# An attention and Fourier-mixer kernel: the weighted sum of the previous step stands on TensorE behind the third pair of tiles of a step, in place of behind the second

## The chip, the cores and the metric

One core of a Trainium2 chip runs the whole program. The metric is the device time of one execution in microseconds (us). Before the change the median of three runs is 1471.29 us (1470.57 to 1473.84). The execution that was profiled took 1468.0 us, of which 1466.2 us lie between the first and the last instruction.

## The reference, cut to what matters

```python
def _L0_conv_ref(x, w_qkv, w_o):           # 8 images of 1024 tokens, 192 channels
    qkv = xt @ w_qkv                       # 12 heads of 16
    attn = softmax(einsum('bhqd,bhkd->bhqk', q, k) * scale)
    out = einsum('bhqk,bhkd->bhqd', attn, v)
    out = out.swapaxes(1, 2).reshape(bs, n, c) @ w_o
...
def _L1_conv_ref(x, w1, b1, w2, b2, bias_w, bias_b):
    bias = x @ bias_w.T + bias_b
    xf = rfftn(x in 4 blocks of 48 channels, axes=(1, 2))
    ...                                    # two small complex layers per frequency, relu between
    return irfftn(...) + bias
...
x = x + _L0_conv_ref(_gn(x), ...)          # _gn: group norm over 32 groups
x = x + _L1_conv_ref(_gn(x), ...)
```

## The kernel before, in words

The program goes through eight images (`b`), and TensorE does each image in 48 steps (`u`, from 0), 16 for each of three groups of four heads. A step has four score tiles, `score_tile(b, g, s, 0..3)`, each of 128 keys by 512 queries for one head; ScalarE takes the exponential of each into `probs`. The score tiles rotate through three banks, so score tile n waits for the exponential of tile n-3.

A step also has four max tiles, `max_tile` 0 to 3. They are tiles of the same products for a stretch of work 11 steps ahead, and VectorE takes the maximum of each row (`take_max`, L1053). They rotate through a ring of four banks, together with everything else that needs a bank: the "pieces". `bank_free` makes TensorE wait until the entry four places earlier in the ring was read out.

TensorE runs a score tile and a max tile in the two halves of its rows at once, so the tiles come in pairs. This document calls them A (max 0 with score 0), B (max 1 with score 1), C (score 2 with max 2) and D (score 3 with max 3). Each reads 48 or 50 rows, and so do, with 64 rows, the small products `qk`, `v`, `proj` and `lin` (all L1340). Everything else on TensorE uses its full height.

The weighted sum of a step, `pv` (W in this document, L1317), multiplies the probabilities of its four score tiles by v and adds into `o_acc`. It is done one step late: W of step u-1 stands in step u. Its four products lie beside each other in the array's columns and use all 128 rows.

The pieces prepare the next image ("prep": turn, mean, var, qk, v) and finish the image before ("post": proj, turn, mean, var, spread, dftw, dfth, mix1, mix2, idfth, idftw, lin). The tables `PREP_AT` and `POST_AT` give for each step the pieces ahead of pair A (START) and those in the middle of the step (MID); `qk`, `v`, `proj` and `lin` come two at a time. With full height, these stand in the middle: prep `var` in step 11, post `var` in 19, `dftw` 2 in 27, `dfth` 0 and 1 in 30, `idftw` 1 in 6 and `idftw` 3 in 7. The `v` pieces of steps 32 and 37 stand there too. `qk` pieces stand ahead of pair A in steps 17, 19, 23, 27 and 32. Each `qk` piece is read out twice: ScalarE copies it (L967), then VectorE subtracts the rounded copy (L1106), and only then is the bank free. The `lin` and `proj` pieces are read by VectorE, the `v` pieces by ScalarE (L961).

Steps 3, 8, 20, 21, 24 and 43 have no pieces. Transposes of the joined row maxima (L1304, `turn_shift`) stand behind pair D of steps 5, 13, 21, 29, 37 and 45. VectorE does the pieces ahead of pair A before the row maxima 0 and 1 of the step. ScalarE does a step in the order: pieces ahead of A, exponentials 0 and 1, at the first step of a group the copy of `o_acc` (`take_o`, L949), MID pieces, exponentials 2 and 3. At the ninth step of a group `take_o` comes first. In all, the loop runs 384 steps. All engines run their instructions in program order, which is written out by hand as shown.

Of the kernel before, what the change touches and what calls it, by code (L numbers as in the profile page):

```python
# [47 lines left out]
START, MID = 0, 1  # L48
# [210 lines left out]
def build(nc, consts, x, w_qkv, w_o, w1, b1, w2, b2, bias_w, bias_b, out):  # L259
# [3 lines left out]
    with ctx:  # L263
# [139 lines left out]
        def after(eng, s, count):  # L403

            if not isinstance(count, int) or count > 0:
                eng.wait_ge(s, count)
# [56 lines left out]
        def ring_bank(entry):  # L463
            return ring[:, RING_NO[entry] % RING, :]
# [26 lines left out]
        def pieces_of(b, u, part, prep, post):  # L491

            late = post and not (isinstance(b, int) and b < 2)
            return [e for e in pieces_at(u, part)
                    if (prep if e[0] == "prep" else late if e[1] == 2 else post)]
# [24 lines left out]
        def max_unit(unit, i):  # L520

            half, m = divmod(unit, HUNITS)
            hp, qt = divmod(m, NT // 2)
            return half, hp, qt, 1 - i % 2, i // 2

        def max_bank(b, g, unit, i):

            if b == 0 and g == 0 and unit < AHEAD:
                return ring[:, i, :]
            return ring_bank(("max", (STEPS * g + unit - AHEAD) % IN_BODY, i))  # L530
# [13 lines left out]
        def halves(b, g, half):  # L544

            return 2 * NG * b + 2 * g + half
# [696 lines left out]
        def _(pe):  # L1243
            mm = nc.tensor.matmul

            def score_tile(b, g, s, h):
                n = g * TILES + s * GH + h
                half, kt = divmod(s, NT)
                if kt == 0 and h == 0:
                    pe.wait_ge(shift_in, 64 * (halves(b, g, half) + 1))  # L1250

                after(pe, probs_made, NG * TILES * b + n + 1 - SCORE_BANKS)
                hp, odd = divmod(h, 2)
                rows = slice(64 * odd, 64 * odd + KQ + 2)
                mm(scores[:, n % SCORE_BANKS, :], k_stack[rows, 2 * g + hp, P * kt:P * (kt + 1)],  # L1255
                   q_stack[rows, g, half, hp, :],
                   start=True, stop=True).then_inc(scores_made, 1)

            def bank_free(b, entry):

                held = bank_held(b, entry)
                if held is None:
                    return
                of, (which, *what) = held
                if isinstance(of, int) and of < 0:
                    pe.wait_ge(max_taken, 4 * (AHEAD - 1) + RING_NO[entry] % RING + 1)
                    return
                if which == "max":
                    g, unit = divmod(what[0] + AHEAD, STEPS)
                    pe.wait_ge(max_taken, TILES * (NG * of + g) + 4 * unit + what[1] + 1)  # L1270
                if which == "turned":
                    pe.wait_ge(shift_split, 2 * halves(*next_half(of, what[0])) + 2)
                if which == "prep":
                    prep_taken(pe, of - what[0], *what[1:])
                if which == "post" and isinstance(of, int) and of == 0:
                    pe.wait_ge(setup_taken, SETUP_TAKEN[SETUP_IN.index(held[1])])
                elif which == "post":
                    post_taken(pe, of - what[0], *what[1:])

            def max_tile(body, u, slot, b, g, unit, i):  # L1280
                half, hp, qt, odd, which = max_unit(unit, i)
                no = 4 * unit + i
                if unit == 0 and i == 0:
                    pe.wait_ge(stacked[g], STACK_INCS * (b + 1))
                if unit == HUNITS and i == 0:
                    pe.wait_ge(stacked_second[g], SECOND_INCS * (b + 1))

                if body == -1:
                    after(pe, max_taken, no + 1 - RING)
                else:  # L1290
                    bank_free(body, ("max", u, i))
                rows = slice(64 * odd, 64 * odd + KQ)
                mm(max_bank(b, g, unit, i),  # L1293
                   q_stack[rows, g, half, hp, P * qt:P * (qt + 1)],
                   k_stack[rows, 2 * g + hp, HALF * which:HALF * (which + 1)],
                   start=True, stop=True).then_inc(max_made, 1)
# [252 lines left out]
            def body(b, prep, post):  # L1549
                first = isinstance(b, int) and b == 0  # L1550

                def pieces(u, part):
                    for which, back, kind, k in pieces_of(b, u, part, prep, post):
                        entry = (which, back, kind, k)
                        bank_free(b, entry)
                        if kind not in PAIRED:
                            (prep_piece if which == "prep" else post_piece)(
                                b - back, kind, k, ring_bank(entry))
                        elif k % 2:
                            (prep_pair if which == "prep" else post_pair)(  # L1560
                                b - back, kind, k, (ring_bank((which, back, kind, k - 1)),
                                                    ring_bank(entry)))
                    for stage, bank_ in setup_of(u, part, first):
                        bank_free(b, SETUP_IN[stage - 1])
                        setup(stage, bank_)

                for u in range(IN_BODY):
                    g, s = divmod(u, STEPS)
                    tiles = unit_ahead(b, u, prep)
                    pieces(u, START)  # L1570
                    for tile in tiles[0:1]:
                        max_tile(b, u, *tile)
                    score_tile(b, g, s, 0)
                    for tile in tiles[1:2]:
                        max_tile(b, u, *tile)
                    score_tile(b, g, s, 1)
                    if s > 0:
                        pv(b, g, s - 1)
                    elif g > 0:
                        pv(b, g - 1, STEPS - 1)  # L1580
                    elif not first:
                        pv(b - 1, NG - 1, STEPS - 1)
                    pieces(u, MID)
                    score_tile(b, g, s, 2)
                    for tile in tiles[2:3]:
                        max_tile(b, u, *tile)
                    score_tile(b, g, s, 3)
                    for tile in tiles[3:]:
                        max_tile(b, u, *tile)
                    if u in shift_steps(prep):  # L1590
                        turn_shift(b, u, *next_half(b, u))
# [74 lines left out]
```

## Time and profile before

| what | value |
|---|---|
| runs, median (lowest to highest) | 1471.29 us (1470.57 to 1473.84) |
| profiled execution | 1468.0 us, span 1466.2 us |
| mean granted TensorE clock | 0.984 |
| TensorE matmul busy | 1402.4 us, 96% |
| VectorE busy | 1153.8 us, 79% |
| ScalarE busy | 1010.8 us, 69% |
| GpSimd busy | 187.9 us, 13% |

Matmul records overlap (two of a pair run at once, and their ends are modelled), so the distance from one start to the next says more than the length of a record. A row of the timeline merges consecutive records of one kind on one engine: its start, the time to the end of the last of them, and behind the shapes how many there are. A product in plain float32 has two records, a pair's tile one.

### The profile page before, as it was taken

The numbers are of one execution on the slowest core, as the hardware profiler recorded it, in microseconds if no ns is written. First come the engines' busy times: TensorE is split into PE (matmuls) and PEld (weight loads), VectorE is DVE, ScalarE is ACT, GpSimd is POOL, SyncE is SP. The second block draws the span as 40 slices with busy tenths as digits, with TensorE's granted clock in tenths as the row PEclk, the third lists the DMA queues.
The fourth block names the chain that finished last, engine by engine and source line by source line (L and its number), as shares of the span: only waits on it lengthen the run. The fifth ranks groups of instructions, "written<-read, shape, count | busy, mean of one in ns | idle before, by whom it ended". The sixth has DMA issues, their size and how long they took to land.

```text
span 1466.2 us, 27125 instructions
## 1 busy us (share of the span) xinstructions
PE 1402.4 (96%) x9852; PEld 668.4 (46%) x9852; DVE 1153.8 (79%) x2123; ACT 1010.8 (69%) x2018; POOL 187.9 (13%) x277
## 2 busy tenths in 40 slices
PE   7899989999999999999999999999999999999977
PEld 4434333444444444444545454444445454434454
DVE  4788888997799878987799878988799878988041
ACT  1166777777767777777777777677777777677712
POOL 2000000040011200140001300140010400040000
PEclk8699999999999999999999999999999999999999
DMA  6610321233530533323422524324432424311323
GB/s 127 88 25 11 79 73 34 52 91 67 109 84 22 106 85 75 74 73 76 104 74 45 107 68 88 80 58 78 109 71 43 87 74 85 88 33 44 82 44 89
DMA packets 100605, 106.35 MB, mean 73 GB/s; under 512 B 24760, under 2 KB 77560, under 8 KB 100472
## 3 DMA queue, kind: packets, MB, share of 16 engines
q1 hardware_dynamic: 98584, 102.98, 32.6%
q10 hardware_dynamic: 1888, 1.63, 0.6%
q8 instruction: 79, 1.29, 0.4%
q14 instruction: 54, 0.44, 0.1%
HBM read 26.99 MB, written 6.67 MB: 23 GB/s over the span
## 4 chain that ended last, share of the span: by engine, by line
PE 81%; DVE 10%; issue 2%; ACT 2%; DMA 1%; POOL 1%; ACTq 0%; SPq 0%; DVEq 0%; POOLq 0%
PE o_acc L1317 23%; PE ring L1293 16%; PE scores L1255 15%; PE ring L1340 10%; DVE row_max L1053 8%; PE ring L1329 3%; PE ring L1451 2%; PE ring L1444 2%; PE ring L1438 2%; PE ring L1357 2%; PE ring L1430 2%; PE ring L1457 1%; DVE qk_parts L1106 1%; ACT probs L941 1%; PE scores L1340 1%
## 5 line engine op out<-in xcount | busy, mean ns | idle before, releaser
L1053 DVE TENSOR_REDUCE row_max<-ring 128x1 f32<-128x512 f32 x1536 | 973.4, 682 | 173.1 <-PE ring L1293 166.9
L941 ACT ACTIVATE probs<-scores 128x512 f32<-128x512 f32 x1536 | 830.0, 599 | 253.9 <-PE scores L1255 252.4
L1293 PE MATMUL ring<-k_stack,q_stack 48*128 48x512 f32 x1536 | 597.3, 465 | 27.8 <-DVE row_max L1053 17.1
L1255 PE MATMUL scores<-q_stack,k_stack 50*128 50x512 f32 x1536 | 598.3, 462 | 1.3 <-ACT probs L941 1.2
L1317 PE MATMUL o_acc<-probs,v_aug 128*18 128x512 f32 x3072 | 406.2, 601 | 4.7 <-ACT o_raw L949 3.6
L1255 PEld LDWEIGHTS scores<-q_stack,k_stack 50*128 50x128 f32 x1536 | 244.3, 185 | 312.6 <-ACT probs L941 298.2
L1293 PEld LDWEIGHTS ring<-k_stack,q_stack 48*128 48x128 f32 x1536 | 248.3, 187 | 153.3 <-DVE row_max L1053 103.9
L584 POOL TENSOR_TENSOR inv_all<-o_raw,inv_all 128x1024 f32<-128x1024 f32 x23 | 54.5, 2371 | 565.0 <-DMA inv_all<-inv_rows 565.0
L1317 PEld LDWEIGHTS o_acc<-probs,v_aug 128*18 128x18 f32 x3072 | 52.0, 96 | 124.1 <-issue 83.8
L1340 PE MATMUL ring<-xt,w_qk 64*128 64x256 f32 x540 | 69.2, 385 | 0.8 <-DVE xt L1092 0.8
L1340 PEld LDWEIGHTS ring<-xt,w_qk 64*128 64x128 f32 x540 | 54.2, 189 | 11.8 <-DVE row_max L1053 3.8
L967 ACT CAST qk_parts<-ring 128x256 fp32r<-128x256 f32 x90 | 29.4, 375 | 41.6 <-PE ring L1340 40.6
L1106 DVE TENSOR_TENSOR qk_parts<-ring,qk_parts 128x256 fp32r<-128x256 f32 x90 | 34.1, 416 | 25.0 <-ACT qk_parts L967 24.6
L881 POOL COPY v_aug<-v_new 128x512 f32<-128x512 f32 x24 | 14.4, 621 | 243.8 <-ACT v_new L961 213.9
L981 ACT COPY rows_a<-ring 128x384 f32<-128x384 f32 x59 | 28.5, 484 | 19.6 <-PE ring L1457 9.6
L836 POOL TENSOR_TENSOR calc<-mean_var,calc 128x1 f32<-128x1 f32 x16 | 3.1, 191 | 299.5 <-DVE calc L1128 212.8
L1451 PE MATMUL ring<-mix_b,spec_a 97*128 97x96 f32 (+1 forms) x304 | 37.2, 274 | 0.7 <-ACT spec_a L989 0.7
L1451 PEld LDWEIGHTS ring<-mix_b,spec_a 97*128 97x128 f32 (+1 forms) x304 | 33.2, 176 | 8.5 <-issue 7.4
L1125 DVE TENSOR_TENSOR x<-ring,x 128x192 f32<-128x192 f32 x60 | 18.7, 352 | 23.0 <-PE ring L1340 23.0
L1438 PE MATMUL ring<-cst,rows_b 128*96 128x128 f32 x240 | 33.2, 286 | 3.3 <-DMA rows_b<-rows_a 3.3
L1340 PE MATMUL ring<-bias_t,xt 64*128 64x192 f32 x360 | 36.3, 326 | 0.0
L1340 PE MATMUL ring<-wo,o_t 64*128 64x192 f32 x366 | 35.2, 322 | 1.0 <-DVE tok_n L1132 1.0
(159 smaller groups left out, 1020.2 us busy)
## 6 DMA issues: line engine op xcount, KB each, us to landing
k_stack<-qk_parts SPq DMA_DIRECT2D x144, 128.0 KB, 4.4
q_stack<-qk_parts SPq DMA_DIRECT2D x285, 64.0 KB, 2.2
inv_all<-inv_rows SPq DMA_DIRECT2D x23, 512.0 KB
rows_b<-rows_a SPq DMA_DIRECT2D x122, 96.0 KB, 3.0
x_in<-in_x_dram SPq DMA_DIRECT2D x8, 768.0 KB, 5.3
x_res<-in_x_dram SPq DMA_DIRECT2D x8, 768.0 KB, 5.3
spec_b<-spec_a SPq DMA_DIRECT2D x60, 102.0 KB, 2.3
o_t<-inv_all SPq DMA_DIRECT2D x184, 32.0 KB, 2.3
```

The source lines that it names most:

```text
L584: ops.tensor_tensor(inv_all[:, :], o_raw[:, :], inv_all[:, :], ALU.mult).then_inc(o_normed, 1)
L941: nc.scalar.activation(probs[:, GH * (s % 2) + h, :], scores[:, n % SCORE_BANKS, :], ACT.Exp, scale=SCALE).then_inc(probs_made, 1)
L967: nc.scalar.copy(qk_parts[:, 0, PARTS[k // 4], token_quarter(k)], bank_[:, 0:QUARTER]).then_inc(part0_done, 1)
L1053: nc.vector.tensor_reduce(row_max[:, which, m:m + 1], max_bank(b, g, unit, i), AX.X, ALU.max).then_inc(max_taken, 1)
L1106: nc.vector.tensor_tensor(qk_parts[:, 1, PARTS[k // 4], cols], bank_[:, 0:QUARTER], qk_parts[:, 0, PARTS[k // 4], cols].bitcast(F32), ALU. ...
L1255: mm(scores[:, n % SCORE_BANKS, :], k_stack[rows, 2 * g + hp, P * kt:P * (kt + 1)], q_stack[rows, g, half, hp, :], start=True, stop=True). ...
L1293: mm(max_bank(b, g, unit, i), q_stack[rows, g, half, hp, P * qt:P * (qt + 1)], k_stack[rows, 2 * g + hp, HALF * which:HALF * (which + 1)], ...
L1317: last = mm(o_acc[32 * h:32 * h + VW, 0, :], v_aug[:, g, kt, h, :], probs[:, GH * (s % 2) + h, :], start=(kt == 0), stop=(kt == NT - 1), s ...
L1329: last = mm(bank_[ROWS * half:ROWS * (half + 1), P * t:P * (t + 1)], src[:, t + NT // 2 * half, third::THIRDS], ident, start=True, stop=True)
L1340: out.append(mm(banks[half][:, 0:n], lhs, rhs, start=(c == 0), stop=(c == 2)))
L1438: last = mm(bank_[0:CH, P * n:P * n + f.shape[1]], rows_b[:, j, CH * chunk:CH * (chunk + 1)], f, start=True, stop=True)
L1451: last = mm(to[:, :, blk, :], hidden[:, blk, P * k:P * k + n], mix_b[:, blk, :], start=True, stop=True)
```

## The change

In the TensorE part of `body`, the MID pieces, score tile 2 and max tile 2 move ahead of the weighted sum. Nothing is added or taken away, and no other engine's order changes.

```diff
                     for tile in tiles[1:2]:
                         max_tile(b, u, *tile)
                     score_tile(b, g, s, 1)
+                    pieces(u, MID)
+                    score_tile(b, g, s, 2)
+                    for tile in tiles[2:3]:
+                        max_tile(b, u, *tile)
                     if s > 0:
                         pv(b, g, s - 1)
                     elif g > 0:
                         pv(b, g - 1, STEPS - 1)
                     elif not first:
                         pv(b - 1, NG - 1, STEPS - 1)
-                    pieces(u, MID)
-                    score_tile(b, g, s, 2)
-                    for tile in tiles[2:3]:
-                        max_tile(b, u, *tile)
                     score_tile(b, g, s, 3)
```

A step was `[START] A B W [MID] C D` and is `[START] A B [MID] C W D`.

Step 27 of an image in the middle of the program, on TensorE: `qk` products (L1340), pairs A and B, W (L1317), `dftw` 2 (L1430), pairs C and D. Before:

```order
L1340 MATMUL ring<-xt,w_qk 128x256 x6
L1293 MATMUL ring<-k_stack,q_stack 128x512
L1255 MATMUL scores<-q_stack,k_stack 128x512
L1293 MATMUL ring<-k_stack,q_stack 128x512
L1255 MATMUL scores<-q_stack,k_stack 128x512
L1317 MATMUL o_acc<-probs,v_aug 18x512 x4
L1430 MATMUL ring<-tok_n,cst 128x384
L1255 MATMUL scores<-q_stack,k_stack 128x512
L1293 MATMUL ring<-k_stack,q_stack 128x512
L1255 MATMUL scores<-q_stack,k_stack 128x512
L1293 MATMUL ring<-k_stack,q_stack 128x512
```

And of the changed kernel, the same place:

```order
L1340 MATMUL ring<-xt,w_qk 128x256 x6
L1293 MATMUL ring<-k_stack,q_stack 128x512
L1255 MATMUL scores<-q_stack,k_stack 128x512
L1293 MATMUL ring<-k_stack,q_stack 128x512
L1255 MATMUL scores<-q_stack,k_stack 128x512
L1430 MATMUL ring<-tok_n,cst 128x384
L1255 MATMUL scores<-q_stack,k_stack 128x512
L1293 MATMUL ring<-k_stack,q_stack 128x512
L1317 MATMUL o_acc<-probs,v_aug 18x512 x4
L1255 MATMUL scores<-q_stack,k_stack 128x512
L1293 MATMUL ring<-k_stack,q_stack 128x512
```

The `dftw` product now stands between two pairs, and W between two others.

Step 32 of the same image on TensorE, in the changed kernel: `qk` products, A, B, the `v` products (L1340, `wv`), C, W, D, and then the first `dfth` products (L1438) of step 33. Before, the row of L1317 stood directly ahead of the row with `wv`.

```order
L1340 MATMUL ring<-xt,w_qk 128x256 x6
L1293 MATMUL ring<-k_stack,q_stack 128x512
L1255 MATMUL scores<-q_stack,k_stack 128x512
L1293 MATMUL ring<-k_stack,q_stack 128x512
L1255 MATMUL scores<-q_stack,k_stack 128x512
L1340 MATMUL ring<-wv,xt 128x192 x6
L1255 MATMUL scores<-q_stack,k_stack 128x512
L1293 MATMUL ring<-k_stack,q_stack 128x512
L1317 MATMUL o_acc<-probs,v_aug 18x512 x4
L1255 MATMUL scores<-q_stack,k_stack 128x512
L1293 MATMUL ring<-k_stack,q_stack 128x512
L1438 MATMUL ring<-cst,rows_b 96x128 x7
```

The `v` products are now directly behind pair B, and the last thing ahead of pair D is W.

## Rows read from the trace of the kernel before

**Rows 1.** The page: span, busy time and share of each engine, instructions.

```profile
span 1466.2 us, 27125 instructions
PE 1402.4 (96%) x9852; PEld 668.4 (46%) x9852; DVE 1153.8 (79%) x2123; ACT 1010.8 (69%) x2018; POOL 187.9 (13%) x277
```

**Rows 2.** Timeline of TensorE, fifth image, from pair C of step 2.

```profile
740.93 0.50 PE L1255 MATMUL scores<-q_stack,k_stack 50*128 50x512 f32 x1
...
741.27 0.62 PE L1255 MATMUL scores<-q_stack,k_stack 50*128 50x512 f32 x2
741.50 0.62 PE L1293 MATMUL ring<-k_stack,q_stack 48*128 48x512 f32 x2
742.11 0.50 PE L1255 MATMUL scores<-q_stack,k_stack 50*128 50x512 f32 x1
742.60 1.05 PE L1317 MATMUL o_acc<-probs,v_aug 128*18 128x512 f32 x8
743.58 0.50 PE L1255 MATMUL scores<-q_stack,k_stack 50*128 50x512 f32 x1
...
743.92 0.39 PE L1255 MATMUL scores<-q_stack,k_stack 50*128 50x512 f32 x1
744.25 1.12 PE L1329 MATMUL ring<-cst,x_in 128*64 128x128 f32 x16
```

**Rows 3.** Timeline of ScalarE, the same stretch; in brackets idle time before.

```profile
741.46 2.07 ACT L941 ACTIVATE probs<-scores 128x512 f32<-128x512 f32 x4 [0.75 <-PE scores L1255]
```

**Rows 4.** Timeline of TensorE, step 2 of that image: A, B and W.

```profile
739.02 0.53 PE L1255 MATMUL scores<-q_stack,k_stack 50*128 50x512 f32 x1
...
739.52 0.49 PE L1255 MATMUL scores<-q_stack,k_stack 50*128 50x512 f32 x1
739.94 1.05 PE L1317 MATMUL o_acc<-probs,v_aug 128*18 128x512 f32 x8
```

**Rows 5.** Timeline of VectorE, the same step.

```profile
738.17 1.29 DVE L1053 TENSOR_REDUCE row_max<-ring 128x1 f32<-128x512 f32 x2 [0.30 <-PE ring L1293]
739.39 0.62 DVE L1125 TENSOR_TENSOR x<-ring,x 128x192 f32<-128x192 f32 x2
```

**Rows 6.** Timeline of TensorE, fourth image, step 23: B and D.

```profile
643.14 0.40 PE L1255 MATMUL scores<-q_stack,k_stack 50*128 50x512 f32 x1
...
644.79 0.40 PE L1255 MATMUL scores<-q_stack,k_stack 50*128 50x512 f32 x1
```

**Rows 7.** Timeline of VectorE, the same step.

```profile
643.62 0.76 DVE L1106 TENSOR_TENSOR qk_parts<-ring,qk_parts 128x256 fp32r<-128x256 f32 x2 [0.72 <-ACT qk_parts L967]
644.29 2.48 DVE L1053 TENSOR_REDUCE row_max<-ring 128x1 f32<-128x512 f32 x4
```

**Rows 8.** Timeline of TensorE, step 27: B, then the middle piece.

```profile
655.60 0.40 PE L1255 MATMUL scores<-q_stack,k_stack 50*128 50x512 f32 x1
...
656.90 0.91 PE L1430 MATMUL ring<-tok_n,cst 128*128 128x384 f32 x2
```

**Rows 9.** Timeline of VectorE, step 27.

```profile
656.18 0.75 DVE L1106 TENSOR_TENSOR qk_parts<-ring,qk_parts 128x256 fp32r<-128x256 f32 x2
```

**Rows 10.** Timeline of TensorE, step 32: B, the `v` products, the next step's `dfth`.

```profile
673.58 0.40 PE L1255 MATMUL scores<-q_stack,k_stack 50*128 50x512 f32 x1
...
674.95 1.21 PE L1340 MATMUL ring<-wv,xt 64*128 64x192 f32 x11
...
676.61 0.57 PE L1438 MATMUL ring<-cst,rows_b 128*96 128x128 f32 x3
```

**Rows 11.** Timeline of ScalarE, step 32: `take_o`, then the `v` pieces.

```profile
675.07 0.62 ACT L949 COPY o_raw<-o_acc 128x512 f32<-128x512 f32 x1
676.24 0.54 ACT L961 COPY v_new<-ring 128x192 f32<-128x192 f32 x2 [0.55 <-PE ring L1340]
```

**Rows 12.** Timeline of TensorE, fourth image, step 9: W and its wait.

```profile
595.32 1.05 PE L1317 MATMUL o_acc<-probs,v_aug 128*18 128x512 f32 x8 [0.43 <-ACT o_raw L949]
```

**Rows 13.** Waits of the whole span: who, for whom, us in total, times, longest.

```profile
PEld ring L1293 <- DVE row_max L1053: 103.9, 253, 1.6
```

## The prediction

> **What bounds the kernel now.** I read the page first: TensorE is busy 96% of the span, VectorE 79% [rows 1]. Then the timeline of TensorE by starts, since its records overlap, and beside it the timelines of VectorE and ScalarE to see who frees a bank when. Last the table of waits.
>
> The reader is to see a fixed cadence in the starts [rows 2]. C starts at 740.93, D at 741.27: 0.34 us, as the first pair behind something of full height. The next pair follows 0.23 behind (741.50). From the last pair of a run to a full-height product it is 0.33 (743.92 to 744.25). From W to the next pair it is 0.98 (742.60 to 743.58). So a run of n pairs between full-height products costs 0.67 + 0.23 (n - 2), and to cut one run in two costs 0.34 + 0.33 - 2 x 0.23 = 0.21 us; a run of one pair is 0.44 by this (0.42 seen, 739.52 to 739.94 [rows 4]). W and the pairs never run together.
>
> TensorE still waits in two kinds of step, both times at B. In steps without pieces the run is C D A B, and B's score tile needs the exponential of C's: it starts at 742.11, 0.61 behind its forerunner instead of 0.23, just behind the first of the four exponentials that began at 741.46, 0.59 each by the distance of scores [rows 2, 3]. W follows at 742.60, 0.05 later than a lone pair asks for, held by D's exponential. In steps that begin with two small products (`proj`, `lin`), B starts 0.50 behind A (739.02, 739.52), because its bank is that of the previous D, whose maximum ends at 739.46 [rows 4, 5]. So a bank freed is a pair started 0.06 later. W stands behind B and waits with it.
>
> **The change, part by part.** It moves each W behind C, and with that the MID pieces ahead of W. No work is added. I count per image, against the 1468.0 us of the profiled execution.
>
> *Runs.* With full-height pieces at START, the runs {C D} {A B} become {D} {A B C}: two runs and four pairs either way, so 0. Without them C D A B becomes D A B C, one run either way, 0. A full-height MID piece stood beside W and cut nothing; now it stands between B and C, and a third run appears: 0.21 each. There are 40 such places in the program (7 images each for `var`, `var`, `dftw` 2, `dfth`; 6 for the two `idftw`): 8.4 us if nothing else happens.
>
> By the Trainium skill, TensorEngine Tiling (Array Packing), Key Properties, a change of tiling mode drains TensorE. The change adds one switch of mode at each of these places, as my count of runs does; if the drain were the pair's 0.50 record less 0.23, the 40 places would cost 10.8 us in place of 8.4.
>
> *Steps without pieces.* In the run D A B C, C's score tile needs the exponential of D's, which is again the first of the run. The wait moves from B to C with its size; only W's own 0.05 goes. Cycle before: 742.60 - 740.93 + 0.98 = 2.65; after: 1.18 + 0.44 + 0.98 = 2.60 [rows 2]. Gain 0.05 in six steps.
>
> *Small products at START.* D's maximum now has the whole run to be done, so B no longer waits (0.27). But C's max tile takes the bank of the first small product, and it comes 0.23 behind B instead of 1.2. VectorE reads the two in 0.62, from 739.39 [rows 5], so the first is free at 739.70, C starts at 739.76 instead of 739.48: 0.28 lost. Net 0 for eight `proj`/`lin` steps; two `v` steps gain 0.05 each. Where VectorE is behind its work at that moment (steps 13 and 29, with a normalisation ahead of them) I take 0.3 and 0.15 of loss; 0.13 for the `v` pieces of step 37.
>
> *`qk` at START.* Here the read-out is a ScalarE copy and then a VectorE subtraction. In step 23 B starts at 643.14, C could start at 643.37, but the first subtraction ends at 644.00 (643.62, two in 0.76) [rows 6, 7]. So C starts at 644.06, W at 644.50, D at 645.48; before, D started at 644.79. Loss 0.69. W used to lie on this wait and hide it; it is 0.98 long and the wait 0.7, so all of it was hidden. Late next: D's exponential, and with it C of step 24, by the same amount. The four row maxima that VectorE does from 644.29 on [rows 7] show that it is behind here, so part of the lateness is absorbed where TensorE waited for VectorE anyway: in steps 17 to 22 I take two `qk` losses of 0.70 and 0.77 (the latter with `var` and its cut), less 0.10 for two steps without pieces, less 0.27 twice for the waits at B of steps 18 and 22: 0.83. Steps 23 and 24: 0.69 - 0.05.
>
> *Step 27*, `qk` and `dftw` 2 in the middle: its bank is that of the first `qk` piece, free at 656.55 (656.18, two in 0.75) [rows 9]. Behind B (655.60) it could start at 655.93 [rows 8]; it starts at 656.61, and 0.21 for the cut: 0.89.
>
> *Step 32*, `qk` and `v` in the middle, is the dearest. The `v` products wait for both `qk` banks: 1.24 behind B as in step 23 (643.14 to 644.38), so 674.87 instead of 673.81. They take 0.98 with C's start at 675.85; W starts at 676.29, D at 677.27, the next piece at 677.7 instead of 676.61 [rows 10]. And this is the first step of a group: ScalarE's `take_o` waits for this W and the `v` copies queue behind it. Before, it started 1.17 behind W's start of 673.90 (675.07) and the copies were free of it. Now it starts at 677.46, ends at 678.05, the first `v` copy ends at 678.3 [rows 11], and the first `dfth` product of step 33, which takes that bank, starts at 678.4: 1.75 late.
>
> *MID elsewhere.* Step 7 loses 0.21. Steps 6, 11 and 30 lose 0.21 and get back the 0.2 that B waited there: 0.
>
> *Steps 8 and 9.* W of step 9 waited 0.43 for `take_o` [rows 12]. W of step 8 comes later, but D's exponential earlier relative to it, and C now stands ahead of W of step 9: 0.40 gained.
>
> Sum for an image with both kinds of pieces: 0.83 + 0.64 + 0.89 + 1.75 + 0.58 + 0.21 = 4.90 lost; 0.40 + 0.15 (steps 3, 8, 43) + 0.10 = 0.65 gained. Net 4.25 over seven images: 29.8 us, from which I take 2 because the first image has no post pieces, so that TensorE waits more there anyway and its step 33 needs no `v` bank. That makes 1468.0 + 28 = 1496; the median of the runs stands 3.3 above the profiled execution, and I say 1498.
>
> **Rivals.**
>
> *The moved wait is absorbed.* Everything late behind a `qk` piece is caught up where TensorE would have waited anyway, and only the 40 cuts cost: +8.4 - 3.2 for step 9 = 1471.3 + 5 = 1476. For it: VectorE is 79% busy and behind around steps 17 to 24. Against it: behind steps 27 and 32 come full-height steps with the bare cadence of rows 2, and there is no wait to fall into.
>
> *Faster.* The waits at B go and nothing takes their place, because C's max tile finds its bank free: VectorE gets to it sooner than I think, or C's score tile keeps the array busy alone. Ten steps with small products (0.27) and six without pieces (0.45) make 5.4 per image, 40 us over seven and a half: 1431. That TensorE waits for row maxima 253 times for 103.9 us [rows 13] leaves room for it. The point that decides is whether the bank of the first small product is free within 0.17 of B's start (C follows 0.23 behind B, and 0.06 of it are the release). I put it at 0.45 in the `lin` step (739.70 against a B at 739.25) and at 0.86 in the `qk` step (644.00 against 643.14), so `lin` is nearer to the edge [rows 4 to 7]. If only `lin` and `proj` gained, that is 8 x 0.27 x 7 = 15 us, and the sum would be 1483.
>
> *No change.* Losses and gains of some 15 us each cancel: 1471. Nothing ties them together.
>
> That the order does not change as said is excluded by the rows of order.
>
> **How the numbers follow.** Forecast as summed: 0.76, with a range of its own from 1484 (half of the loss of step 32, or all of the gain in `lin` steps) to 1508 (no absorption in steps 17 to 24, 0.54 an image or 4 us, and another 0.1 in the ten small-product steps of each image, 7 us). Absorbed: 0.12. Faster: 0.07. No change: 0.05. The range is 1476 to 1508: it takes in my own sum's low side and the middle of the absorbed case, and leaves the two rivals below out. A difference of 0.2% is about what a measurement of this kernel can tell from no change. The part of the absorbed case and of my own that falls below is small: faster 0.08, same 0.06, slower 0.86.
>
> **What the profile of the changed kernel would show.** In steps without pieces, the fourth pair of the run late by 0.4 still. In `lin` steps B 0.23 behind A, and C late. In `qk` steps C's max tile 0.9 behind B, waiting for L1106. Step 27: `dftw` about 1.0 behind B. Step 32: `take_o` and the `v` copies ahead of a late first L1438. W of step 9 nearly without its wait. VectorE's and ScalarE's busy times the same. I would be wrong if C's wait in `qk` steps were short, or if pairs standing alone cost more than 0.44.

## The result: slower by 1.6%

The changed kernel takes 1494.31 us (median of three, 1492.67 to 1498.63) against 1471.29: 1.0163 of the time before, 95% interval 1.0138 to 1.0188. The profiled execution is the longest of the three, 1498.63 us. Every ratio in this document is an estimate over all executions beside each other and can differ a little from the quotient of the two medians, most in the run with W between A and B (1.0104, where the medians give 1.0131).

The page of the changed kernel, which answers to [rows 1]. Nobody does more work; the busy times are about as before in a longer span:

```profile
span 1496.8 us, 27125 instructions
PE 1416.8 (95%) x9852; PEld 696.2 (47%) x9852; DVE 1166.5 (78%) x2123; ACT 1022.3 (68%) x2018; POOL 187.3 (13%) x277
```

Timeline of TensorE, fifth image, steps 2 and 3, which answers to [rows 2] and [rows 4]. It begins with pair A of step 2; in brackets the idle time before and who ended it.

```profile
755.94 0.77 PE L1255 MATMUL scores<-q_stack,k_stack 50*128 50x512 f32 x2
756.32 0.39 PE L1293 MATMUL ring<-k_stack,q_stack 48*128 48x512 f32 x1
756.55 0.40 PE L1255 MATMUL scores<-q_stack,k_stack 50*128 50x512 f32 x1
756.73 0.50 PE L1293 MATMUL ring<-k_stack,q_stack 48*128 48x512 f32 x1
757.16 1.05 PE L1317 MATMUL o_acc<-probs,v_aug 128*18 128x512 f32 x8
758.14 0.49 PE L1255 MATMUL scores<-q_stack,k_stack 50*128 50x512 f32 x1
...
759.32 0.50 PE L1255 MATMUL scores<-q_stack,k_stack 50*128 50x512 f32 x1 [0.21 <-ACT probs L941]
...
759.76 1.05 PE L1317 MATMUL o_acc<-probs,v_aug 128*18 128x512 f32 x8
760.74 0.50 PE L1255 MATMUL scores<-q_stack,k_stack 50*128 50x512 f32 x1
```

B (its max tile at 756.32) now starts 0.38 behind A instead of 0.50, and their ends are 0.24 apart instead of 0.46: B no longer waits. C's score tile goes at 756.55, but its max tile waits until 756.73, and W with it. In step 3 the wait has moved from B to C (759.32). From D to D this cycle is 760.74 - 758.14 = 2.60, against 2.65 before.

Timelines of step 23 of the fourth image (`qk` products at its start), TensorE from B on and VectorE, which answer to [rows 6] and [rows 7]:

```profile
656.74 0.40 PE L1293 MATMUL ring<-k_stack,q_stack 48*128 48x512 f32 x1
656.98 0.40 PE L1255 MATMUL scores<-q_stack,k_stack 50*128 50x512 f32 x1
657.70 0.50 PE L1293 MATMUL ring<-k_stack,q_stack 48*128 48x512 f32 x1 [0.32 <-DVE qk_parts L1106]
658.12 1.05 PE L1317 MATMUL o_acc<-probs,v_aug 128*18 128x512 f32 x8
659.11 0.49 PE L1255 MATMUL scores<-q_stack,k_stack 50*128 50x512 f32 x1
```

```profile
657.22 0.76 DVE L1106 TENSOR_TENSOR qk_parts<-ring,qk_parts 128x256 fp32r<-128x256 f32 x2 [1.09 <-ACT qk_parts L967]
```

C's max tile starts 0.96 behind B (656.74 to 657.70) where the cadence allows 0.23: half of the 0.76 of the two subtractions, from 657.22, ends at 657.60, and the trace names L1106 as what ended the wait. W used to stand there.

The waits of TensorE's weight loads over the whole span, which answer to [rows 13]: waits for row maxima fell from 253 and 103.9 us to 88 and 39.1 us. Waits of score tiles for exponentials grew (before: 298.2 us, 371 times), and those of max tiles for the `qk` subtraction are new (before: 0.2 us, once). Weight loads also wait while earlier matmuls still run, so these sums are not all lost time (TensorE's matmuls are busy for 95% of the span all the same). The last line is of the matmuls themselves: the first `v` product of step 32, about 1.0 us in each of seven images (before: 0.3 us, once).

```profile
PEld scores L1255 <- ACT probs L941: 371.2, 469, 1.1
...
PEld ring L1293 <- DVE row_max L1053: 39.1, 88, 1.1
...
PEld ring L1293 <- DVE qk_parts L1106: 12.7, 17, 1.1
...
PE ring L1340 <- DVE qk_parts L1106: 7.2, 7, 1.3
```

Step 32 on TensorE (the `v` products, C, W, D, the `dfth` products of step 33), which answers to [rows 10]:

```profile
690.17 1.21 PE L1340 MATMUL ring<-wv,xt 64*128 64x192 f32 x11 [0.99 <-DVE qk_parts L1106]
691.09 0.53 PE L1255 MATMUL scores<-q_stack,k_stack 50*128 50x512 f32 x1
...
691.59 1.05 PE L1317 MATMUL o_acc<-probs,v_aug 128*18 128x512 f32 x8
692.57 0.49 PE L1255 MATMUL scores<-q_stack,k_stack 50*128 50x512 f32 x1
...
693.57 2.10 PE L1438 MATMUL ring<-cst,rows_b 128*96 128x128 f32 x16 [0.50 <-ACT v_new L961]
```

And on ScalarE, which answers to [rows 11]:

```profile
692.71 0.58 ACT L949 COPY o_raw<-o_acc 128x512 f32<-128x512 f32 x1 [2.27 <-PE o_acc L1317]
693.19 0.55 ACT L961 COPY v_new<-ring 128x192 f32<-128x192 f32 x2
```

ScalarE stood idle for 2.27 us, because `take_o` is ahead of the `v` copies in its queue and waited for W. The `v` products were ready for about the last 1.25 us of it: in the run below whose ScalarE order lets the copy go first, it starts 1.29 behind their start.

**Where the time went, step by step.** The times at which the score tiles' semaphore rises give the distance from the end of pair D to the end of D of the next step. What follows is the median over images 3 to 7 of this distance, changed kernel less kernel before, in us; steps not named differ by 0.03 or less:

| steps | difference |
|---|---|
| 2, 10, 11, 12, 29, 36 | +0.06, +0.06, +0.05, +0.06, +0.06, +0.03 |
| 3, 8, 20, 21, 24, 43 | -0.05 or -0.06 each |
| 7 | +0.19 |
| 9 | -0.48 |
| 13, 14 | +0.35, -0.10 |
| 17, 18 | +0.59, -0.43 |
| 19, 22, 23, 25 | +0.76, -0.05, +0.82, -0.07 |
| 27 | +0.83 |
| 32, 33 | +1.17, +0.56 |
| 37, 38 | +0.26, -0.33 |
| sum of all 48 | +4.08 |

Over the eight images of the profiled execution it is 4.5, 3.9, 4.2, 4.1, 4.1, 3.5, 4.1 and 1.0, in all 29.4 us of the 30.6 between the two profiled executions (1498.63 less 1468.0). The last image prepares no next one and has no `qk` pieces. The 4.5 of the first image holds about 2.7 us that are not of this kind; the paragraph on the first image below takes them apart.

### The profile page after: what moved, and what is told of

The parts are those of the page before. It is cut to its first block, busy times and chain, and to the rows that moved or that the text cites. A ratio compares the mean times of both kernels' runs of the same rounds, so it can differ in the third digit from the quotient of the medians.

```text
span 1496.8 us, 27125 instructions
## 1 busy us (share of the span) xinstructions
PE 1416.8 (95%) x9852; PEld 696.2 (47%) x9852; DVE 1166.5 (78%) x2123; ACT 1022.3 (68%) x2018; POOL 187.3 (13%) x277
## 3 DMA queue, kind: packets, MB, share of 16 engines
q8 instruction: 79, 1.29, 0.4%
## 4 chain that ended last, share of the span: by engine, by line
PE 83%; DVE 7%; ACT 4%; issue 2%; DMA 2%; ACTq 0%; SPq 0%; POOL 0%; DVEq 0%; POOLq 0%
PE o_acc L1317 24%; PE scores L1255 19%; PE ring L1293 12%; PE ring L1340 10%; DVE row_max L1053 5%; PE ring L1329 3%; ACT probs L941 2%; PE ring L1451 2%; PE ring L1438 2%; PE ring L1444 2%; PE ring L1357 2%; PE ring L1430 2%; DVE qk_parts L1106 1%; PE ring L1457 1%; ACT qk_parts L967 1%
## 5 line engine op out<-in xcount | busy, mean ns | idle before, releaser
L1293 PE MATMUL ring<-k_stack,q_stack 48*128 48x512 f32 x1536 | 624.4, 471 | 21.0 <-DVE row_max L1053 7.4
L1255 PE MATMUL scores<-q_stack,k_stack 50*128 50x512 f32 x1536 | 589.1, 459 | 13.1 <-ACT probs L941 12.9
L1255 PEld LDWEIGHTS scores<-q_stack,k_stack 50*128 50x128 f32 x1536 | 260.7, 186 | 393.3 <-ACT probs L941 371.2
L1317 PE MATMUL o_acc<-probs,v_aug 128*18 128x512 f32 x3072 | 406.5, 601 | 0.7 <-ACT probs L941 0.7
L1293 PEld LDWEIGHTS ring<-k_stack,q_stack 48*128 48x128 f32 x1536 | 267.1, 188 | 127.1 <-DVE row_max L1053 39.1
L1317 PEld LDWEIGHTS o_acc<-probs,v_aug 128*18 128x18 f32 x3072 | 51.6, 96 | 114.4 <-issue 72.0
L1340 PE MATMUL ring<-xt,w_qk 64*128 64x256 f32 x540 | 67.1, 382 | 0.8 <-DVE xt L1092 0.8
L1106 DVE TENSOR_TENSOR qk_parts<-ring,qk_parts 128x256 fp32r<-128x256 f32 x90 | 34.4, 419 | 34.3 <-ACT qk_parts L967 33.0
L967 ACT CAST qk_parts<-ring 128x256 fp32r<-128x256 f32 x90 | 29.4, 375 | 45.5 <-PE ring L1340 43.1
L1340 PEld LDWEIGHTS ring<-xt,w_qk 64*128 64x128 f32 x540 | 53.7, 190 | 8.8 <-issue 2.3
L949 ACT COPY o_raw<-o_acc 128x512 f32<-128x512 f32 x48 | 28.0, 583 | 24.2 <-PE o_acc L1317 24.2
L1340 PE MATMUL ring<-wv,xt 64*128 64x192 f32 x336 | 33.4, 330 | 7.6 <-DVE qk_parts L1106 7.2
L1438 PE MATMUL ring<-cst,rows_b 128*96 128x128 f32 x240 | 33.8, 290 | 6.3 <-DMA rows_b<-rows_a 3.3
```

The costliest lines, as they stand in the source:

```text
L967: nc.scalar.copy(qk_parts[:, 0, PARTS[k // 4], token_quarter(k)], bank_[:, 0:QUARTER]).then_inc(part0_done, 1)
L1106: nc.vector.tensor_tensor(qk_parts[:, 1, PARTS[k // 4], cols], bank_[:, 0:QUARTER], qk_parts[:, 0, PARTS[k // 4], cols].bitcast(F32), ALU. ...
L1293: mm(max_bank(b, g, unit, i), q_stack[rows, g, half, hp, P * qt:P * (qt + 1)], k_stack[rows, 2 * g + hp, HALF * which:HALF * (which + 1)], ...
L1317: last = mm(o_acc[32 * h:32 * h + VW, 0, :], v_aug[:, g, kt, h, :], probs[:, GH * (s % 2) + h, :], start=(kt == 0), stop=(kt == NT - 1), s ...
L1340: out.append(mm(banks[half][:, 0:n], lhs, rhs, start=(c == 0), stop=(c == 2)))
L1438: last = mm(bank_[0:CH, P * n:P * n + f.shape[1]], rows_b[:, j, CH * chunk:CH * (chunk + 1)], f, start=True, stop=True)
```

## The experiments

All experiments use the kernel before with one table: at which step W stands where. 0 is between A and B, 1 between B and C ahead of the MID pieces (as before), 2 between score tile 2 and max tile 2, 3 behind C (as in the change).

```diff
+                    def weigh(place):
+                        if W_AT.get(u, 1) != place:
+                            return
...
                     score_tile(b, g, s, 0)
+                    weigh(0)
...
                     score_tile(b, g, s, 1)
+                    weigh(1)
                     pieces(u, MID)
                     score_tile(b, g, s, 2)
+                    weigh(2)
                     for tile in tiles[2:3]:
                         max_tile(b, u, *tile)
+                    weigh(3)
```

The step differences given below are read as in the table above, always against the kernel before. The times that follow "against" are medians of the kernel before, run beside the others.

### Only the five steps with `qk` at the start

```diff
+W_AT = {17: 3, 19: 3, 23: 3, 27: 3, 32: 3}
```

> W stands behind C (as in the changed kernel) in the five steps with qk pieces ahead of A (17, 19, 23, 27, 32), and between B and C, as before the change, in the other 43. Theory (in these steps C's max tile, or the middle piece, waits for a bank that VectorE has not yet read out, and W no longer covers that wait): nearly the whole loss, about 4 us for an image with qk pieces, seven of them, so 26 to 30 us more than before: 1497 to 1501 us. Rival (the loss is spread over all steps, by the cuts of the runs and by pairs that stand alone): five of 48 steps, so under 10 us more than before.

Measured: 1497.18 us against 1469.91, ratio 1.0185 (1.0159 to 1.0211). Five of 48 steps are enough for the whole loss, 3.9 us an image: 17 and 18 +0.78 - 0.51, 19 and 20 +0.74 - 0.25, 23 and 24 +0.82 - 0.25, 27 +0.93, 32 and 33 +1.17 + 0.56.

### All steps but those five

```diff
+        if W_AT.get(u, 3) != place:
+W_AT = {17: 1, 19: 1, 23: 1, 27: 1, 32: 1}
```

> The complement: W behind C in 43 steps, and as before the change in the five steps with qk pieces ahead of A. Theory: the losses of step 7 (0.2), 13 (0.35) and the small ones of the steps with proj or lin are paid back by steps 8 and 9, so within 3 us of the kernel before: 1468 to 1474 us. Rival (loss spread over all steps): most of the 23 us, 1485 us or more.

Measured: 1474.7 us against 1469.91, ratio 1.0033 (1.0015 to 1.0051). Just above the stated 1474, and far from the rival's 1485. The steps named in the expectation came as in the changed kernel, but four others lost: 18, 20 and 24 by 0.28, 0.20 and 0.29, which all follow a step whose W stands in the middle, and 30 by 0.43. (Steps 17 and 19, with W in the middle behind a step with W behind C, gained 0.13 and 0.08.) In step 30 TensorE now stands at its `dfth` products earlier by the length of W, and at times ahead of the transfers that they read. The waits of L1438 for the DMA of `rows_b` are 5.3 us over 4 times, against 3.3 us once before; that is 2.0 us of the 2.9 that the first seven images lost there, the rest is not named. The loss is not the same in all of them: nothing in three, 0.4 to 1.2 in four. The two complementary runs lose 27.3 and 4.8 us, more together than the 23.0 of the change, since what a step loses depends on where W stands in the step ahead of it.

```profile
PE ring L1438 <- DMA rows_b<-rows_a: 5.3, 4, 3.3
```

### Step 32 alone, and the same with ScalarE's order changed

```diff
+W_AT = {32: 3}
```

> W behind C in step 32 alone. Theory (the v products wait for both qk banks, and then ScalarE's copy of o_acc waits for the late W with the copies of the v products queued behind it, so that the first dfth product of step 33 waits for its bank): 1.2 us late at pair D of step 32 and another 0.55 at the dfth product of step 33, 1.75 an image, 12 us in all: 1481 to 1485 us. Rival (only the wait for the qk banks): 0.7 to 1.2 an image, 1476 to 1479 us.

Measured: 1482.44 us, ratio 1.0093 (1.0067 to 1.0118); step 32 +1.17, step 33 +0.54. One step of 48 costs about half of what the whole change costs.

The second kernel has this on ScalarE in addition:

```diff
+                    for piece, *job in jobs_of(b, u, MID, prep, post, prep_piece, post_piece):
+                        piece(*job)
                     if s == 0 and not (first and g == 0):
                         take_o(slot - 1, 1)
-                    for piece, *job in jobs_of(b, u, MID, prep, post, prep_piece, post_piece):
-                        piece(*job)
```

> As the run with W behind C in step 32 alone, and on ScalarE the pieces in the middle of a step stand ahead of the copy of o_acc (take_o) at the first step of a group. That frees the v banks before W is done. Theory: the second part of the loss goes, 0.55 an image, so 3 to 5 us faster than the run before this one, and pair D of step 32 is still 1.2 us late: 1477 to 1481 us. Rival (the second part comes from the exponentials being late, or from W itself): no difference between the two runs.

Measured: 1476.47 us, ratio 1.0065 (1.0041 to 1.0088), a little below the stated range; step 32 +1.16, step 33 nothing. Its timeline of ScalarE shows the `v` copies ahead of the copy of `o_acc`:

```profile
684.56 0.54 ACT L961 COPY v_new<-ring 128x192 f32<-128x192 f32 x2 [1.03 <-PE ring L1340]
685.79 0.59 ACT L949 COPY o_raw<-o_acc 128x512 f32<-128x512 f32 x1 [0.69 <-PE o_acc L1317]
```

So the 0.55 of step 33 is shown to be ScalarE's queue behind `take_o`. The 1.17 of step 32 stays, so it is not that queue. The trace gives about 1.0 of it to the `v` products' wait for the second `qk` subtraction (0.99 in the fence of step 32 above, 0.98 in this kernel). That is read from the traces; no run took this wait away.

### Is it the max tile's bank?

```diff
+W_AT = {17: 2, 19: 2, 23: 2}
```

> In steps 17, 19 and 23 (qk pieces ahead of A) W stands between score tile 2 and max tile 2, so the score tile of C goes ahead of W and the max tile, which takes the bank of the first qk piece, behind it; all other steps as before the change. Read by the distance from pair D of the step before to pair D. Theory (it is the max tile's bank that is late, not the score tile): the 0.7 to 0.8 is gone and what stays is the broken pair, 0.23 in steps 17 and 23, 0.23 plus the cut of 0.21 plus the wait of var for the first qk bank, 0.3 to 0.5, in step 19. Rival (ScalarE is late with the score banks because of its qk copies): steps 17 and 23 still 0.6 to 0.8 longer.

Measured, in one execution of 1482.02 us: step 17 +0.20, step 23 +0.22, each followed by -0.19 and -0.24 in the next, so that nothing is left; step 19 +1.01, with -0.25 in step 20. Timeline of TensorE in step 23: score tiles 1 and 2, W, then max tile 2.

```profile
645.50 0.63 PE L1255 MATMUL scores<-q_stack,k_stack 50*128 50x512 f32 x2
646.06 1.05 PE L1317 MATMUL o_acc<-probs,v_aug 128*18 128x512 f32 x8
647.05 0.50 PE L1293 MATMUL ring<-k_stack,q_stack 48*128 48x512 f32 x2
```

Score tile 2 passed without a wait, and max tile 2 found its bank free at 647.05. The late thing in steps 17 and 23 is the bank of the max tile, not ScalarE with the score banks. Step 19 lost more than the 0.74 to 0.94 that I had put for it. Its `var` product stands ahead of W here as well, and in the fourth image it starts 0.91 behind B (at 632.23) instead of 0.33:

```profile
633.14 0.38 PE L1350 MATMUL ring<-calc,cst 128*128 128x1 f32 x2 [0.52 <-DVE qk_parts L1106]
```

So the wait for the first `qk` bank is 0.58, where I had 0.3 to 0.5; with 0.23 and 0.21 that is 1.02.

### Full-height pieces in the middle

```diff
+W_AT = {6: 3, 7: 3, 11: 3, 30: 3}
```

> W behind C in steps 6, 7, 11 and 30 alone, the four with full-height pieces in the middle and no qk at their start. Read by the distance from pair D to pair D. Theory (the middle piece now cuts the run of A, B, C): step 7 0.19 to 0.21 longer, as in the changed kernel; step 11 the same 0.2, because its wait at B stays and only the cut is added; step 30 waits for the transfers of rows_b that its dfth products read, since these land about when its B starts: 0.3 to 0.6 longer. Rival (a full-height piece beside the pairs costs nothing of its own): 0.05 or less in steps 7 and 11.

Measured, in one execution of 1476.29 us: step 7 +0.20, step 11 +0.19, step 30 +0.37, step 6 +0.37. The cut of a run costs what [rows 2] gave, 0.21 less 0.01 or 0.02. But the steps behind 7 and 11 gave it back, 8 -0.25 and 12 -0.22, which I had not foreseen: in step 12 B's wait is gone, and in step 8 the run is D A B, without a fourth pair that waits for ScalarE. In the changed kernel, where steps 8 and 12 have their W behind C too, step 7's 0.19 stays.

Step 30 is in its range, but mostly not for my reason. Steps 6 and 30 lost the same, and step 6 reads no such transfer. Step 6 in the fifth image on TensorE (B, then the `idftw` product) and VectorE:

```profile
754.20 0.50 PE L1255 MATMUL scores<-q_stack,k_stack 50*128 50x512 f32 x1
754.79 0.91 PE L1357 MATMUL ring<-rows_b,cst 128*128 128x384 f32 x2
```

```profile
752.76 1.97 DVE L1053 TENSOR_REDUCE row_max<-ring 128x1 f32<-128x512 f32 x3
```

The product's bank is that of pair D of step 5, whose maximum ends at 754.73, and it starts 0.06 later: 0.59 behind B, where W stood 0.43 behind B before. That is the second 0.16. In step 30 it is the same (the maximum ends at 836.40, L1438 starts at 836.46). The transfers come on top in some images only: L1438 waits for them 4 times here (4.5 us against 3.3 us once), and images 2, 4 and 7 lost 0.5 to 0.7 in step 30 where 3, 5, 6 and 8 lost 0.34 to 0.37.

### Only the steps where it gained

```diff
+W_AT = {3: 3, 8: 3, 9: 3, 20: 3, 21: 3, 24: 3, 25: 3, 43: 3}
```

> W behind C only in steps 3, 8, 9, 20, 21, 24, 25 and 43: the steps without pieces, and the two where W waits for the copy of o_acc. Theory: 0.05 in each of the six steps without pieces, 0.48 in step 9, nothing given back: 0.7 to 0.85 an image, 5 to 7 us faster than before: 1464 to 1466 us. Rival (in these steps too the wait only moves and turns up in the next one): within 2 us of before.

Measured: 1468.16 us against 1469.72, ratio 0.9989 (0.9974 to 1.0005). My theory fell here. A step without pieces with W behind C is 0.05 or 0.06 shorter only when the step ahead has its W there too (21: -0.06). Where the step ahead has W in the middle it is 0.18 to 0.28 longer (3, 8, 20, 24, 43): the run is then C D A B C, five pairs, and the fourth and fifth wait for ScalarE. But steps 10, 22 and 44, behind such a step and with their own W in the middle, got 0.22 to 0.25 shorter, which I had not foreseen: their wait at B was gone.

### W earlier, between A and B

```diff
+W_AT = {2: 0, 10: 0, 12: 0, 13: 0, 18: 0, 22: 0, 29: 0, 36: 0, 39: 0, 44: 0, 47: 0}
```

> The other direction: W between A and B in eleven steps where B waits for the bank of the previous D (2, 10, 12, 13, 29, 36, 39, 44, 47 with small products ahead of A, and 18 and 22), between B and C elsewhere. Theory (0.98 us of W covers B's wait of 0.25 to 0.35, and nothing new is late: the count of runs is the same): 0.22 in nine steps and 0.35 in two, 2.7 an image, 17 to 21 us faster: 1450 to 1454 us. Rival (VectorE is the bound of these stretches, so the wait turns up at C or D or at the next step's A): under 5 us faster.

Measured: 1488.97 us, ratio 1.0104 (1.0066 to 1.0141). The rival was right. Ten of the eleven steps got 0.17 to 0.31 shorter, as expected, and the next one gave it back and more where it begins with small products, `qk` or a transposed maximum: 11 +0.42, 13 +0.45, 19 +0.60, 23 +0.68, 30 +0.34. (Step 13 is itself the eleventh.) Step 3, without pieces, got +0.29 by a run of five pairs, B C D A B. Timeline of TensorE, step 10 (A, W, B C D) and the `proj` products of 11:

```profile
609.00 0.53 PE L1255 MATMUL scores<-q_stack,k_stack 50*128 50x512 f32 x1
...
609.46 1.05 PE L1317 MATMUL o_acc<-probs,v_aug 128*18 128x512 f32 x8
...
610.45 0.73 PE L1255 MATMUL scores<-q_stack,k_stack 50*128 50x512 f32 x2
...
611.82 1.21 PE L1340 MATMUL ring<-wo,o_t 64*128 64x192 f32 x11 [0.40 <-DVE row_max L1053]
```

Three max tiles now come in one go and VectorE needs 0.6 for each (2.48 for four in [rows 7]), so the next small products wait for it. By steps this comes to 0.6 us an image. Most of the 19 us of the medians is something else, which the last section shows.

> Both tables at once: W between A and B in the eleven steps, behind C in the eight, between B and C elsewhere. Theory: the gains add up, 3.4 to 3.5 an image, 22 to 28 us faster than before: 1443 to 1449 us. Rival (they share a wait): no faster than the better of the two alone.

Measured, with both tables at once: 1481.03 us, ratio 1.0079 (1.0049 to 1.0109), 1.0 us an image over the kernel before. The gains do not add up since one of them was none; its numbers by step are those of the two tables: 9 -0.47, 3 +0.48, 11 +0.44, 19 +0.59, 23 +0.67.

### W behind C just ahead of the steps that wait

The surprise in steps 10, 22 and 44 gives a rule of its own: put W between C and D of the step ahead, so that VectorE has one row maximum left behind W instead of two, and leave W in the middle of the step that begins with small products. First step 9 alone:

```diff
+W_AT = {9: 3}
```

> W behind C in step 9 alone. Theory: step 9 gets 0.43 to 0.48 shorter, because the copy of o_acc is done when W comes; and step 10, which begins with two proj products, loses its wait at B (0.23), because with W between C and D of step 9 only one row maximum is left behind the pair that B's bank belongs to. 0.7 in each of eight images, 5 to 6 us: 1464 to 1465 us where the kernel before has 1470. Rival (the row maxima only come later, or step 9's gain belongs to W of step 8 standing behind C too): 0.25 an image or less, under 2 us.

Measured: 1468.41 us against 1471.0, ratio 0.9975 (0.9958 to 0.9992). Step 10 -0.22 as expected; step 9 only -0.13, so 0.36 an image, between theory and rival, and the median is above the stated 1465. The rival had the part of step 9: of the 0.48 that the change gains there, most comes only if step 8's W stands behind C too. In the run with eight steps above it did, and steps 8 and 9 together came to 0.19 - 0.47.

```diff
+W_AT = {1: 3, 9: 3, 12: 3, 20: 3, 21: 3, 28: 3, 35: 3, 38: 3, 46: 3}
```

> W behind C in the steps just ahead of those that begin with small products (1, 9, 12, 28, 35, 38 and 46), and in 20 and 21 (ahead of the spread of 22); elsewhere as before the change, in the steps with small products too. Theory: VectorE has only D's row maximum behind W instead of C's and D's, so the next step's B finds its bank free: 0.22 less in steps 2, 10, 13, 29, 36, 39 and 47, 0.47 less in step 9, 0.1 less for steps 20 to 22; nothing is lost, since full-height pieces or a wait already stand at the start of these steps. 2.0 to 2.1 an image, 14 to 17 us: 1453 to 1456 us. Rival (VectorE is the bound there, the wait turns up a step later, as it did with W between A and B): 0.7 an image, that of step 9 and 10 alone, 1464 us or more.

Measured: 1463.96 us against 1471.0, ratio 0.9943 (0.9922 to 0.9965): faster than both kernels, by half of what I had expected: 1.3 us an image. Steps 2, 10, 13, 22, 29, 36, 39 and 47 are each 0.21 to 0.24 shorter. Timeline of TensorE, step 1's W and D, then the `lin` products and A and B of step 2:

```profile
739.71 1.05 PE L1317 MATMUL o_acc<-probs,v_aug 128*18 128x512 f32 x8
740.69 0.50 PE L1255 MATMUL scores<-q_stack,k_stack 50*128 50x512 f32 x1
...
741.88 0.77 PE L1255 MATMUL scores<-q_stack,k_stack 50*128 50x512 f32 x2
...
742.58 1.05 PE L1317 MATMUL o_acc<-probs,v_aug 128*18 128x512 f32 x8
```

W follows A's start by 0.70 where [rows 4] have 0.92 (739.02 to 739.94). What was given back: 0.13 instead of 0.47 in step 9; step 20 +0.19 by the run of five; step 35 +0.15, not taken apart; and step 32 +0.34 in the median, nothing in some images and 0.3 to 0.6 in four. In three of images 4 to 7 TensorE comes to the first score tile of step 32 before the shifts that SyncE sends for it have landed (1.6 us of such waits, 0.2 us before), and once in image 3 (0.3 us). The waits of that stretch, 560 to 1240 us:

```profile
PEld scores L1255 <- DMA q_stack<-shift: 1.6, 3, 0.6
```

## Why the prediction was right

**The sum.** Forecast: 4.25 us an image with both kinds of pieces; measured 4.08. Forecast 1498, measured 1494.31, inside the range of 1476 to 1508. The difference of the medians is 23 us and that of the profiled executions 30.6, so most of the gap to my 26.7 and 28 is which executions were met.

That the sum came so near is in part luck: two terms missed by 0.3 to 0.4 an image each and cancelled, the sum for steps 13, 29 and 37 (0.58 forecast, 0.23 measured with what 14 and 38 give back) and that for the other small products (a gain of 0.10 forecast, a loss of 0.31 measured). Two slips of arithmetic are smaller: the times put for step 32 give 678.4 - 676.61 = 1.79 and not 1.75, and the top of the range adds up to 1498 + 11 = 1509 and not 1508.

**Cadence.** That to cut a run costs 0.21 was right: 0.19 or 0.20 in step 7 in three kernels, and 0.19 in step 11 in the run on full-height pieces, where the next step gave it back. Steps 6, 11 and 30 came to 0.01, 0.05 and 0.01 in the changed kernel, where I had 0. A pair alone takes 0.43 (760.74 to 761.17 in the trace of the changed kernel), as rows 2 and 4 gave.

By the Trainium skill, TensorEngine Tiling (Array Packing), Key Properties, a change of tiling mode drains TensorE. The steps with a cut agree that an added switch is paid for, with 0.19 to 0.20 and not the 0.27 of my estimate from the whole record.

**Steps without pieces.** Right in the changed kernel, to 0.01. The runs showed that this holds only while the neighbouring steps are changed too.

**Small products at START.** The mechanism was right (B's wait gone, C's max tile late), the term was a little off: +0.06 in steps 2, 10, 11 and 12 where I had 0. C's wait cost what I had put: W stands 1.22 behind A in the changed kernel (755.94 to 757.16), and the 0.70 that A and B take without a wait (the last kernel of the experiments), plus 0.23 for C, make 0.93, so 0.29. B's wait was smaller than my 0.27: where it is gone, B starts 0.38 behind A and not 0.23, and W comes only 0.22 earlier (0.70 for 0.92). For 13 and 29 I had 0.3 and 0.15 and it is 0.25 (with what 14 gives back) and 0.06; for 37 I had 0.13, and with step 38 it is -0.07.

**`qk` at START.** The term that made the sign, and it held: 0.69 - 0.05 = 0.64 predicted for steps 23 and 24, 0.77 measured. What was absorbed in steps 17 to 22 I had put at 0.27 each at steps 18 and 22; it was 0.43 in step 18 and 0.05 in 22. The stretch has 0.76 where I had 0.83.

**Steps 27 and 32.** 0.83 for 0.89, and 1.73 for 1.75, its two parts told apart by the runs with step 32. For the 0.83 and for the first part of the 1.73, the cause (the `qk` bank) is read from the traces; the run that moved the max tile alone shows it for steps 17 and 23.

**Steps 8 and 9.** 0.53 gained with step 8's 0.05, for 0.40 and 0.05. Sign and size were right; that the bulk of it hangs on step 8 came out only in the run with step 9 alone. (`take_o` stands first on ScalarE in the steps numbered 9, 25 and 41 from 0.)

**First image.** I took 2 us off for it, and it lost 4.5 us, as much as any. But 3.1 of the 4.5 stand in steps 11 to 13, where TensorE ran at half clock for longer than in the trace of before (the last section); in the later images these steps come to 0.45, so 2.7 less. In the run with the five `qk` steps, whose stretch at half clock there is as long as before (6.8 us), the first image lost 2.7 where the next six lost 3.4 to 4.0. And step 33 changed by 0.1 or less in the first image, in these two kernels and with step 32 alone, where later images lost 0.5 to 0.6, as I had said. So the deduction had its cause right and was about the right size: 1.3 us by this run, 2.2 by the changed kernel less the 2.7; what I had not reckoned with is the clock.

**The rivals.** The absorbed case is out: where full-height steps follow (27, 32) nothing came back. The faster one is out for `lin` and `proj` by the 0.18 of C's max tile behind its score tile and by their +0.06, and for `qk` by a wide margin.

## What to carry to other kernels

An in-order engine's long piece of independent work is also a cover: look at which bank or buffer becomes free while it runs, and what would stand waiting without it. Count what comes behind it on every other queue that waits for its end. And a step's best place for such a piece depends on where its neighbours have theirs, since what matters is how many products are left for the slower engine between two of its deadlines; take the sum over a pair of steps, and not over one.

## What the runs showed that I had not expected

TensorE's granted clock falls to half in the first image for a time that differs between the traces. Windows of 20 us with the busy time of each engine and, third from the end, the mean granted clock (PEclk), kernel before:

```profile
100.00:120.00 20.00, 17.84 (x136) 8.78 (x134) 14.63 (x29) 10.18 (x19) 2.33 (x10) 0.86 0.00 1
120.00:140.00 20.00, 18.69 (x129) 8.62 (x125) 16.67 (x31) 13.67 (x28) 0.00 (x0) 0.97 0.01 3
```

The changed kernel:

```profile
100.00:120.00 20.00, 19.08 (x122) 11.37 (x119) 12.03 (x24) 8.17 (x16) 2.31 (x10) 0.70 0.00 1
120.00:140.00 20.00, 18.97 (x117) 8.17 (x113) 16.46 (x32) 13.57 (x28) 0.00 (x0) 0.96 0.01 3
```

The kernel with W between A and B:

```profile
100.00:120.00 20.00, 18.38 (x106) 11.28 (x102) 9.49 (x20) 6.07 (x13) 1.74 (x7) 0.63 0.00 1
120.00:140.00 20.00, 18.83 (x103) 7.39 (x101) 14.34 (x28) 11.75 (x24) 0.00 (x0) 0.69 0.01 2
```

The clock has two levels, 1.2 and 2.4 GHz, so these means stand for about 7 us at the low one in the kernel before, 14 in the changed kernel and 27 in the last. None of them stood idle for long ahead of it: the longest gaps between matmul records from 85 to 135 us are 1.29, 0.92 and 1.62 us. In these 40 us the last kernel has 209 matmul records where the kernel before has 265. Its first image took 13.0 us more than before, the later ones 0.4 to 1.8 us. Four of its six executions have a mean clock of 0.970 to 0.972 and 1488.5 to 1490.1 us, the other two 0.980 and 0.983 and 1478.9 and 1476.0; the kernel before had 0.976 to 0.986 in 17 executions beside it, and 1466 to 1479 us. Why this order meets the low clock more often stays open. It does not explain all of the 15 to 19 us: by the steps of images 2 to 8 this order itself costs 6 us. The profiled execution of the fastest kernel (1468.65 us, the slowest of its six) also has such a stretch, of 24 us; its first image lost 6.3 us, and the other seven gained 8.3 together. For comparisons of a few us here, the distances between like steps of the trace tell more than the totals.
